# Preparing the first batch element's attention inside layer 0, and ranking the scores in two halves

## The reference, cut to what matters

```
scores = (x @ w_imp)[..., 0]
_, idx = top_k(scores, 32);  idx = sort(idx);  sel = x[idx]
a1 = attn(q, k1, v1, causal)   # keys and values from a latent of 32 channels
a2 = attn(q, ks, vs)           # the 32 selected tokens
a3 = attn(q, kw, vw, causal)   # keys and values straight from x
out = (g0*a1 + g1*a2 + g2*a3) @ w_proj,   g = softmax(mean_t(x @ w_gate))
```

## Time and profile before

| | |
|---|---|
| median of 3 runs | 2059.49 us (2054.94 to 2062.57) |
| the profiled execution | 2060.56 us, span 2058.8 us |
| busy in the span | PE 1826.0 us (89%), DVE 1274.1 (62%), ACT 1173.1 (57%), POOL 674.2 (33%) |
| mean granted TensorE clock | 0.932 of full speed |

### The profile page before, as it was taken

The page is one execution under the profiler, slowest core; times in us unless marked ns, Lnnn a source line. Parts: engine busy times, 40 slices in busy tenths (PEclk is TensorE's granted clock), DMA queues, the critical chain, the costliest instruction groups (busy, mean ns, idle before and its releaser), DMA issues.

```text
span 2058.8 us, 38328 instructions
## 1 busy us (share of the span) xinstructions
PE 1826.0 (89%) x10668; PEld 1078.2 (52%) x10668; DVE 1274.1 (62%) x3790; ACT 1173.1 (57%) x3572; POOL 674.2 (33%) x699
## 2 busy tenths in 40 slices
PE   4565559999999999999999999999999999999995
PEld 2233235565555655555555555655565555555552
DVE  4899535656656565656566656566666656665673
ACT  2455215666656565666565656565666656566661
POOL 0345332343334333333233323332343334333300
PEclk8677559999999999999999999999999999999998
DMA  4000021112111211112011111211112111211101
GB/s 154 1 0 0 1 50 47 37 38 51 47 38 37 51 47 27 45 35 57 24 40 41 51 29 41 47 37 48 37 38 50 47 38 37 51 47 37 37 1 41
DMA packets 71347, 81.42 MB, mean 40 GB/s; under 512 B 29522, under 2 KB 37843, under 8 KB 70995
## 3 DMA queue, kind: packets, MB, share of 16 engines
q1 hardware_dynamic: 71122, 78.74, 15.0%
HBM read 7.90 MB, written 2.10 MB: 5 GB/s over the span
## 4 chain that ended last, share of the span: by engine, by line
issue 49%; PE 20%; POOL 18%; DVE 8%; ACT 2%; SPq 1%; POOLq 1%; DMA 0%; DVEq 0%; ACTq 0%
PE bank L1727 6%; PE bank L1754 3%; POOL arena L681 3%; PE bank L1690 3%; POOL arena L683 2%; POOL arena L670 2%; POOL arena L680 2%; POOL arena L671 2%; PE bank L1601 2%; DVE arena L1173 1%; POOL arena L679 1%; POOL arena L719 1%; PE bank L1655 1%; PE bank L1596 1%; PE bank L1638 1%
## 5 line engine op out<-in xcount | busy, mean ns | idle before, releaser
L1400 DVE CUSTOM_DVE_ANT_0 arena<-bank,W 128x512 f32<-128x512 f32 (+3 forms) x1024 | 479.9, 487 | 533.2 <-PE bank L1727 370.6
L972 ACT ACTIVATE arena<-arena 128x512 f32<-128x512 f32 (+3 forms) x1024 | 570.3, 560 | 366.2 <-DVE arena L1400 363.3
L1727 PE MATMUL bank<-arena 96*128 96x512 f32 (+6 forms) x2048 | 719.2, 453 | 24.9 <-issue 15.4
L1727 PEld LDWEIGHTS bank<-arena 96*128 96x128 f32 x2048 | 351.5, 192 | 200.7 <-issue 163.9
L1754 PE MATMUL bank<-W,arena 128*128 128x128 f32 x2560 | 429.4, 282 | 0.3 <-ACT arena L972 0.2
L1754 PEld LDWEIGHTS bank<-W,arena 128*128 128x128 f32 x2560 | 300.2, 143 | 221.9 <-issue 182.3
L1411 DVE COPY arena<-bank 128x512 f32<-128x512 f32 (+1 forms) x512 | 318.3, 622 | 82.2 <-PE bank L1754 79.3
L719 POOL TENSOR_TENSOR arena<-arena,one 128x512 f32<-128x512 f32 x64 | 66.5, 1038 | 812.5 <-DVE arena L1368 806.4
L1690 PE MATMUL bank<-arena 128*32 128x256 f32 (+1 forms) x3072 | 222.6, 362 | 0.9 <-DVE arena L1411 0.7
L972 ACT ACTIVATION_READ_ACCUMULATOR arena<-arena 128x1 f32 x1024 | 197.2, 193 | 0.0
L951 ACT ACTIVATE arena<-bank 128x384 f32<-128x384 f32 x256 | 124.4, 486 | 95.4 <-PE bank L1754 93.5
(11 more groups left out here) (264 smaller groups left out, 2252.7 us busy)
## 6 DMA issues: line engine op xcount, KB each, us to landing
arena<-arena SPq DMA_DIRECT2D x896, 64.0 KB, 2.0
arena<-arena SPq DMA_DIRECT2D x64, 128.0 KB, 2.4
W<-wide SPq DMA_DIRECT2D x1, 3730.0 KB, 13.3
X<-x SPq DMA_DIRECT2D x8, 256.0 KB, 5.5
out<-arena SPq DMA_DIRECT2D x8, 256.0 KB, 2.3
arena<-arena SPq DMA_DIRECT2D x96, 16.0 KB, 1.9
LW<-lat SPq DMA_DIRECT2D x1, 768.5 KB, 14.3
arena<-mods SPq DMA_DIRECT2D x1, 768.0 KB, 4.8
```

What stands on the lines that cost most here:

```text
L972: done = A(here, here, ACT.Exp, bias=nmax[:, c:c + 1], scale=-1.0, accum_out=lsum[:, c:c + 1])
L1400: last = v.tensor_tensor_reduce(Pb[:, s % 4, at_p:at_p + n], bank[turn.score_bank(s)][:, at + lo:at + lo + n], w("mask", T - n), -1.0, 3e3 ...
L1727: last = MM(B_[:, at:at + lo + n], query(t), Kb[a][0:QD, g % 2, h, skip:skip + lo + n], start=True, stop=True)
```

## The change

Five things change; what is computed stays the same.

- **Setup.** `s_setup` is signalled once `modc` is ready. `norm_mix(0)` waits for the first piece of x alone (`s_x0`), and the weight quantisation, the copies of the rows and the `gate_fix` calls stand behind it in DVE's list. POOL's first `gate_wo` waits for a new semaphore `s_rowg`. The scaling of the latent weights and the `gate_fix` of `garow1` move into iteration 0.
- **START goes into layer 0.** The table `SLOTS` gives each projection of START an iteration and a place in it: "top" before `turn_input`, "mid" before `project_out`, "out" before `ffn`, "end" after it. ACT reads at matching places. POOL copies `hTc` in iteration 2 and has `rms` in 3, `shared_key` in 4, `rope` of the queries in 5 and of the keys in 7. DVE normalises the latents in 4.
- **Banks.** Bank 0 takes all three kinds of transposes, with three more waits on PE; bank 7 is free for START and bank 5 for the scores.
- **Scores in two halves.** Each element's score row is made once its `HT` is there, in two sums of four elements in bank 5. The first four are ranked on DVE in iteration 8, which gives element 0's selection; all eight are ranked during `FIRST`, in steps 0 to 12 of its units, and the gates' softmax goes there too (steps 1 and 5).
- **Memory.** The buffers that START fills are carved apart from layer 0's; `Qb`, `Kb` and `V` become lists of one buffer for each parity.

```diff
+SLOTS = {(3, "mid"): "cqkv", (3, "end"): "kr", (4, "end"): "nqT",
+         (5, "mid"): "x1q", (5, "out"): "x2q", (5, "end"): "nq",
+         (6, "mid"): "vw", (6, "out"): "x1k", (6, "end"): "x2k",
+         (7, "mid"): "nk3", (7, "out"): "nk1", (7, "end"): "vl",
+         (8, "end"): "rank", (9, "top"): "sel", (9, "mid"): "ks", (9, "out"): "vs"}
@@ POOL, in the loop over iterations
+                if b == 2:
+                    pool.wait_ge(s_h3, 1)
+                    pool.tensor_copy(hTc, HT[:, 0:T]).then_inc(s_hTc, 1)
+                if b == 3:
+                    step(pool.memset(vsbd, 0.0))
+                    rms(start)
+                if b == 4:
+                    shared_key(start, None)
+                if b == 5:
+                    rope(start, "q", 0)
+                if b == 7:
+                    rope(start, "k", 0)
@@ ACT
+            for b in range(5):
+                row_read(b)
+            act.wait_ge(s_setup, 1)
+            normed_mix(0)
+            for b in range(5, B):
+                row_read(b)
@@ ACT, in the loop
+                slot(b - 1, "end")
+                slot(b, "top")
...
+                slot(b, "mid")
...
+                slot(b, "out")
@@ DVE, the loop over iterations
+                if b == -1:
+                    row_gates(modrow[:, :, 0])
+                if 0 <= b < B:
+                    wkv(b)
+                if b == 4:
+                    norm_latents(0)
+                if b == 6:
+                    scores_copied(HALF_B)
+                if 0 <= b - 1 < B:
+                    quantised_ffn(b - 1)
+                if b == 8:
+                    for n in range(KEEP // 8):
+                        top_found(1)
+                        top_marked()
+                    top_flagged()
+                    top_counted()
+                    top_ranked()
+                if b == 8:
+                    for j in range(NT):
+                        tokens(0, j)
+                if b == 9:
+                    read(start, "rank", 0)
+                    for j in range(NT):
+                        last = pick(0, j)
+                    last.then_inc(s_zc, 1)
+                    read(start, "ks", 0)
+                if 0 <= b + 1 < B:
+                    maxima(b + 1)
+                if b == -1:
+                    row_gates(modrow[:, :, 3])
+                    ffn_rows()
+                if b == 0:
+                    latent_weights()
+                if 0 <= b < B:
+                    norm_ffn(b)
+                if 0 <= b - 2 < B:
+                    keep_moments(b - 2)
+                if 0 <= b + 2 < B:
+                    norm_mix(b + 2)
+                if b == -2:
+                    quantise_weight()
+                    row_reads()
+                    v.wait_ge(s_rowsa, B)
+                if b == 0:
+                    row_gates(garow1[:])
+                    TS(gsm, gmx, 1.0, None, ALU.mult).then_inc(s_gproj, 1)
+                if 0 <= b - 1 < B:
+                    norm_attention(b - 1)
@@ DVE, in attend, for FIRST
+                    if turn.first:
+                        if s == 0:
+                            scores_copied(B)
+                        if s == 1:
+                            gates_shifted()
+                        if s == 5:
+                            gates_normed()
+                        if 2 <= s < 2 + KEEP // 4:
+                            (top_marked if s % 2 else lambda: top_found(2))()
+                        if s == 10:
+                            top_flagged()
+                        if s == 11:
+                            top_counted()
+                        if s == 12:
+                            top_ranked()
@@ PE, the loop over iterations
+            def score(b):
+                pe.wait_ge(s_h3, b + 1)
+                if b == HALF_B:
+                    pe.wait_ge(s_scr, 1)
+                MM(bank[5][0:B], impd[:, b], HT[:, b * T:(b + 1) * T], start=(b % HALF_B == 0), stop=(b % HALF_B == HALF_B - 1)).then_inc(s_sc, 1)
...
+                slot(b, "top")
+                if 0 <= b + 1 < B:
+                    turn_input(b + 1)
+                    project_mixes(b + 1)
+                if 0 <= b - 2 < B:
+                    turn_attention(b - 2)
+                slot(b, "mid")
+                if 0 <= b < B:
+                    project_out(b)
+                slot(b, "out")
+                if 0 <= b - 1 < B:
+                    ffn(b - 1)
+                if 0 <= b - 2 < B:
+                    score(b - 2)
+                slot(b, "end")
+            gate_logits()
```

More of the change, by code:

```diff
@@ L336, in build @@
         inv = cv(2, NT * HG)
[L337 to L341 removed]
+        top, marked = c_st[0:B], gi[0:B]
         onehot = gi[:, 0:P].rearrange("p (j k) -> p j k", j=NT)
@@ L946, in attend @@
                         read(turn, *task)
+                    if turn.first and s == 2:
+                        act.wait_ge(s_gs, 1)
+                        A(gates[:], gates[:], ACT.Exp, scale=1.0 / T).then_inc(s_ge, 1)
                     k = s - T_LAG
@@ L984, in attend, with slot @@
                         selected_keys(turn, s // GU + 1)
[L986 to L993 removed]
+            start = Turn(START)
+            def slot(b, where):
+                name = SLOTS.get((b, where))
+                if name and READER.get(name, "act") == "act":
+                    read(start, name, 0)
+            for b in range(5):
[4 more added lines that the diff above has]
+                row_read(b)
+            for b in range(-2, B + 2):
+                if 0 <= b + 1 < B:
+                    if b + 1 > 0:
+                        normed_mix(b + 1)
+                    mix_input(b + 1)
+                slot(b - 1, "end")
+                slot(b, "top")
+                if 0 <= b - 2 < B:
+                    normed_attention(b - 2)
+                    attention_input(b - 2)
+                if 0 <= b + 1 < B:
+                    receptance(b + 1)
+                slot(b, "mid")
+                if 0 <= b - 1 < B:
+                    ffn_input(b - 1)
+                if 0 <= b + 1 < B:
+                    exponentials(b + 1)
+                slot(b, "out")
+                if 0 <= b < B:
+                    normed_ffn(b)
+            selected_keys(start, 0)
             attend(Turn(FIRST))
@@ L1457, in attend @@
                             cell_new(mark["cell"])
-            turn = Turn(START)
-            for j in range(NT):
-                tokens(0, j)
-            for j in range(NT):
-                last = pick(0, j)
-            last.then_inc(s_zc, 1)
-            v.wait_ge(s_gl, 1)
-            step(CP(gates[:].rearrange("p b n -> p (b n)"), bank[1][:, 0:3 * B]))
-            step.settle()
-            step(v.tensor_reduce(gmx, gates[:], AX_X, ALU.max))
-            step.settle()
-            TT(gates[:], gates[:], gmx.rearrange("p (b o) -> p b o", o=1).to_broadcast([P, B, 3]), ALU.subtract).then_inc(s_gs, 1)
@@ L1616, in fill @@
                     last = MM(G[ROPE:P], w("krsw"), hTc, start=True, stop=True)
+                elif name == "rank":
+                    pe.wait_ge(s_rank, 2 if turn.first else 1)
+                    for j in range(NT):
+                        last = pe.transpose(G[:, j * B:(j + 1) * B], top[:, j * P:(j + 1) * P], ident[0:B, 0:B])
                 elif name == "sel":
```

382 lines of the change are left out of this document (176 added, 206 removed).

## The result

| | before | after |
|---|---|---|
| median | 2060.86 us (4 runs, 2054.94 to 2062.57) | 2010.74 us (4 runs, 2009.01 to 2012.96) |
| profiled execution, span | 2060.56, 2058.8 us | 2012.96, 2011.1 us |
| mean granted clock | 0.932 | 0.947 |

The ratio is 0.9762, with a 95% interval of 0.9740 to 0.9785: 2.4% faster. The forecast was 2015.0 us with a range of 2003 to 2031. In the profiled executions, in which the sum was made, the gain is 47.6 us where 45.5 was forecast; by the medians it is 50.1.

The account below looks back on a forecast made before the run. It took the first 310 us as the place to gain: setup, layer 0's two nearly level chains, and START's serial 68 us. Terms -9.9 + 6.05 + 7.0 - 50.2 + 1.5 = -45.5 from 2060.56 gave 2015.0 us, range 2003 to 2031.

Parts of the forecast that it names:

- Setup, -9.9: Setup up to element 1's scan: reordered lists start that scan 9.9 us earlier, bounds 5 and 13.
- Layer 0, +6.05: Layer 0, iterations 0 to 7: START's added work costs 6.05 us together, bounds 3 and 17.
- the drain, +7.0: Last element: `decode(7)` stands behind the key rotation on POOL, +7.0 us; +4.2 if rotation is free, +9 if colliding throughout.
- Iteration 6: Layer 0: query rotation before `decode(5)`, four score copies on DVE and POOL-DVE interference cost +3.2 us (2 to 6).
- The fear that POOL and DVE exclude each other: Rotations: each of twelve POOL instructions could lose up to one DVE instruction and the reverse; upper end for iteration 6, 6 us.
- Tail, -50.2: From `norm_attention(7)` to the first attention scores: 25.5 us instead of 75.7, and from 241.5 instead of 234.49, -50.2 us.
- FIRST, +1.5: `FIRST`: about 12 us of ranking, copies and gates on DVE cost +1.5 us, between 0 and 6.
- The loop: Attention loop: untouched by the change, turns stay at 231 us; prediction wrong if a turn changes by more than 2 us.
- Rival 4: Attention loop gets slower: decides from 6.5 us a turn (2.8%); at 8 us a turn 2071 us; chance 0.04.
- 1 (the lists give it back): In-order lists: PE's slots at half clock, layer 0 at its upper bound, `FIRST` 6 us: +15, 2030 us; chance 0.17.
- 2: Setup and drain give more: setup 13, rotation half hidden (-3), `FIRST` 0: -8, 2007 us; chance 0.15.
- 3: Tail: chain to the selected keys only moved, ranking or `Kb`'s DMAs stay behind last `HT`: 2036 us; chance 0.09.

Follow-up runs that it names:

- Setup undone: Changed kernel with DVE's and ACT's setup lists put back in the old order; median 2025.08 us, ratio 0.9833 to the kernel before.
- One ranking: Changed kernel with all eight score rows ranked once behind the last `HT`, nothing ranked in `FIRST`; median 2029.02 us, ratio 0.9847 to the kernel before.
- keys first: Changed kernel with PE's `ks` directly behind `sel`, ahead of the last element's transposes; 2006.89 us in one run.
- no ranking in FIRST: Changed kernel without the four max and match-replace rounds, flags and count in `FIRST`; 2013.88 us in one run.
- four edits: Changed kernel with `ks` directly behind `sel`, query rotation split around `decode(5)`, key rotation behind `decode(7)`, selected keys' DMAs on two queues; median 2003.39 us, ratio 0.9724.
- three, no split: Changed kernel with `ks` directly behind `sel`, key rotation behind `decode(7)`, selected keys' DMAs on two queues, query rotation left whole; median 2005.56 us, ratio 0.9724.
- decode first: Changed kernel with POOL's key rotation behind `decode(7)` instead of ahead of it; 2007.19 us in one run.
- query split: Changed kernel with half of POOL's query rotation before `decode(5)` and half behind it; 2008.48 us in one run.

## Why the prediction was right, and where it was off

**Setup, -9.9: right.** The last row is read at 25.65 (said: 26.1), the receptance at 31.83 (32.1), the exponentials end at 36.91 (37.2); the scans stand at 38.36 and 61.39 (38.9 and 61.4). PE's twelve passes took 5.4 us, not 5.2, at 2.4 GHz. *Setup undone* shows the first scan's 14.9 us causally. The work left in iteration 0 was not taken out by itself: between the reciprocals of elements 0 and 1 it is 24.33 us where before has 19.24, +5.1 for the 6.4 less 1.5 of the sum.

**Layer 0, +6.05, and the drain, +7.0: 13.05 forecast, 11.9 measured.** Against their places in the old frame:

| | predicted | measured |
|---|---|---|
| iterations 1 and 2 | 0 | -0.7 |
| 3 | +0.5 | +0.8 |
| 4 | +0.85 | +1.5 |
| 5 | +0.8 | +1.0 |
| 6 | +3.2 | +3.4 |
| 7 and drain | +7.7 | +5.9 |

Each is a difference of reciprocals. Before they are 21.55 us apart from element 2 on, and 22.34 between elements 1 and 2; after they are at 68.96, 90.60, 112.15, 134.53, 157.54, 180.13 and 205.09. Iteration 6 was sized well, though with the wrong weight on its parts. What ended last before the decode was not the rotation but DVE, 2.9 us late with the quantisation: 1.2 for the copies of the scores, 1.2 for L1227 and L1232 beside the rotation, and 0.5 for small instructions (128x16) beside POOL's L676 and L638. But POOL's own list was only 1.04 us from being the bound. *One ranking* has no copies in this iteration, and its decode starts 9.46 us after the reciprocal, only 0.41 sooner than in after: one small instruction (L1084) took 1.14 us there, beside L676, and 0.11 elsewhere. Its interval is 25.72 us even so, as PE passed the bias and the product behind the decode at 1.2 GHz (2.07 us each, 1.12 and 1.16 in after).

The drain was taken as the whole rotation, +7.0, and 0.7 for iteration 7, and that is the term that was too large. The decode ran 2.35 us later than in the earlier trace rows (229.58 against 227.23), as the prediction's 234.3 less 3.85 said within 0.9. From the reciprocal to it are 24.49 us, 6.6 more than before, so the rotation was paid almost in full; but `norm_attention(7)` followed 6.59 us behind the decode where the earlier trace rows have 7.26, as PE had the last `HT` transposes behind it by then (L1624 at 223.50; at 228.48 in before).

The fear that POOL and DVE exclude each other in every instruction was too large. Beside the reciprocal, which has one input, the query rotation's first instructions took their 1.09 us; of all twelve only two were longer, 1.54 each, beside L1227 and L1232, which have two inputs in SBUF. In the drain L1281 and L1285 took 1.64 and 1.95 (0.68 and 1.21 in *one ranking*, where POOL is still). The Trainium skill, SBUF — State Buffer, section "Who interferes with whom", names these pairs, and says that a VectorE instruction with at most one SBUF input doesn't contend outside the two-port modes, which `tensor_scalar` can enter. The trace agrees in the pairs and in the reciprocal; the one-input instructions that did grow beside POOL were TENSOR_SCALARs (L1079, 0.50 us for 0.17, and L1084), in which mode no run here shows. What it costs here is 0.5 to 1.0 us for each of the four DVE instructions.

**Tail, -50.2: -51.4 measured.** It took 24.28 us, not 25.5, so the first scores came at 260.45 (said: 263), with `norm_attention(7)` at 236.17 (237.7) and the first of the twelve DMAs at 250.46 (253.2). `sel` was put at 1.9 us and took 1.05 (L1712). The last element's attention input does wait for the selection in ACT's list, as said; `ks` behind that element's transposes, in PE's list, is the 2.9 us that *keys first* took away. Of the 51.4 us *one ranking* shows 16.6 to be due to the halves. No run puts START's projections and rotations back by themselves; that the rest is due to their move is read from the two timelines.

**FIRST, +1.5: +1.2 measured, for another reason.** The prediction laid it on the max and match-replace steps 2 to 9. These delay units by up to 1.7 us (the seventh on DVE is 12.81 us from the first, and 11.11 in *no ranking in FIRST*) and are caught up again; without them and the count 0.3 goes. What stays arises at steps 12 to 15, from L1289 and the ranks' transposes with their read.

**The loop: unchanged, but wrongly named.** "Each of its turns takes 231 us" was a misreading: 231 was the length of the window, not a turn. By the DVE copy that opens each turn a turn took 215.65 us before (358.87 to 1652.74 over six) and 215.10 after. The change of 0.55 is under the 2 us at which the prediction would have been wrong. Rival 4's price, 6.5 us a turn, did not rest on the 231.

**The rivals.** 1 (the lists give it back) didn't occur: of the slots before `ffn`, those of iterations 5 and 6 took 1.02 to 1.12 us, at 2.4 GHz; at 1.2 GHz (2.07) ran late ones such as `x2k` at 197.40, in PE's idle time, and `vl` at 218.88, and the first of the two of iteration 7 (1.92 us at 207.75), both of which had been put at that clock. 2 was right about the drain in direction (5.9 for 7.7). 3 is what *one ranking* builds: 16.6 us in the tail, against the 21 of the worst case. 4 didn't occur; by the true turn its threshold of 6.5 us is 3.0%, not 2.8%.

## What to carry to other kernels

A serial stretch of some 70 us between two pipelined stages could be moved almost whole into the first stage although one of its engines was full, because the moved work was on the others: 51 us came out for 12 us of delay in the first stage. What such a move costs is read from the wait that ends last after it. Behind one of the two rotations the decode waited for DVE, which the rotation had slowed, and not for the rotation's own end, and putting half of it elsewhere bought nothing. Two pieces of work beside each other cost what the longer costs: 5.8 and 3.5 us alone, 5.9 together. And gains are to be summed over the whole stretch up to the next common point: by their own intervals four edits gave 10.3 us, over the whole stretch the three that count gave 7.7 singly and 7.7 together. The next bound, the gate logits, could be read in the first run in which PE's idle time shrank to 0.9.

## What had not been expected of the hardware

- The same instruction at nearly the same time meets either level of TensorE's clock from run to run. The first reciprocal falls at 44.6 to 45.2 us in some runs and at 46.4 to 47.0 in others (46.1 in *three, no split*), with the same setup code before it. Both begin with the same step, the row product of the third element, in after and in *three, no split*:

```profile
17.49 1.09 PE L1617 MATMUL bank<-arena 128*128 128x512 f32 x2 [1.35 <-DVE small L1164]
```

```profile
17.57 2.04 PE L1622 MATMUL bank<-arena 128*128 128x512 f32 x2 [1.34 <-DVE small L1169]
```

  One is at 2.4 GHz, the other at 1.2, after the same idle time. Iteration 4 does the same: between the reciprocals of elements 4 and 5 it is 23.0 us where the bias (L1662) takes 2.07 us, as in after, and 22.2 where it takes 1.12, as in *decode first*. Those 0.8 us cover the 0.6 that iteration 4 cost beyond the forecast. In a single profile such steps hide an edit of 1 to 2 us, so the parts were compared by intervals. What decides the level was not looked into.
- In *query split* a decode that came 1.2 us earlier met the lower level in the next iteration (2.08 and 1.11 us for passes of 1.64 and 0.66), and 2.0 us were lost there.
- Issuing twelve DMAs of 16 KB from one queue takes 8.11 us; six from each of two take 4.34 and 4.16 side by side.
